# PReLU halves of the background rows merged by VectorE before the transposes, in a graph kernel on one core

## The reference

```
h = prelu(gcn_conv(x, W1, b1), a); h = prelu(gcn_conv(h, W2, b2), a)
x = layernorm(x + h)          # prelu(z) = z where z > 0, else a * z, with an own a for each feature
```

## The kernel before

| offset | engine | step |
|---|---|---|
| 0 | SyncE | `load` of the rows into X (L203) |
| 1 | TensorE | `transpose`, 4 transposes into bank 5 (L229) |
| 2 | ScalarE | `lift` to xt (L238) |
| 3 | TensorE | `mult_first`, 1 matmul (L243) |
| 4 | ScalarE | `rectify_first`: up = relu(z + b), down = relu(-z - b) (L252, L253) |
| 5 | TensorE | `mult_second`: 2 matmuls that add up, up by V2 and down by V2n = -a V2 (L261, L262); in slots jobs also h1 = up + (-a) down by 8 matmuls into bank 7 (L269, L270) |
| 6 | ScalarE | `rectify_second` (in slots jobs first H from bank 7), up and down again (L283, L284) |
| 7 | TensorE | `join`: xt + up + (-a) down by 12 matmuls into bank 7 (L295 to L297) |
| 8 | VectorE, ScalarE | `spread`: statistics (L309, L314, L316); `root` (L324) |
| 9 | VectorE, ScalarE | `invert` (L334, L335); `normal` (L344) |
| 10 | SyncE | `store` (L213); `store_h1` stands at offset 7 |

## Time and profile before

### The profile page before, as it was taken

The page is one execution under the profiler, slowest core; times in us unless marked ns, Lnnn a source line. Parts: engine busy times, 40 slices in busy tenths (PEclk is TensorE's granted clock), DMA queues, the critical chain, the costliest instruction groups (busy, mean ns, idle before and its releaser), DMA issues. The chain is left out here.

```text
span 12483.0 us, 94733 instructions
## 1 busy us (share of the span) xinstructions
PE 5282.3 (42%) x22640; PEld 4046.0 (32%) x22640; DVE 4400.5 (35%) x11160; ACT 3794.3 (30%) x11417; POOL 7315.7 (59%) x7464
## 2 busy tenths in 40 slices
PE   4510572444444444442044444455555553211533
PEld 3300351333323333331033333344444442111532
DVE  7900231232322223345033333334333333233433
ACT  3400461333222222226342222223222222124422
POOL 6777105326666666665655656666666666654556
PEclk7655555555665556655555555555555555555655
DMA  3211221133333333333133333333333333322211
GB/s 51 56 26 23 67 83 40 43 68 81 88 87 83 87 89 88 89 87 105 33 77 80 87 84 87 86 93 95 93 93 94 92 91 88 82 57 55 77 33 32
DMA packets 791340, 920.27 MB, mean 74 GB/s; under 512 B 258978, under 2 KB 676540, under 8 KB 790748
## 3 DMA queue, kind: packets, MB, share of 16 engines
q1 hardware_dynamic: 558638, 591.29, 16.0%
q0 software_dynamic: 232064, 323.36, 13.8%
q10 hardware_dynamic: 144, 0.10, 0.0%
HBM read 533.07 MB, written 388.06 MB: 74 GB/s over the span
## 5 line engine op out<-in xcount | busy, mean ns | idle before, releaser
L1589 POOL DMA_INDIRECT l_g<-tab,l x4704 | 4577.9, 973 | 2674.7 <-issue 1343.1
L1794 DVE TENSOR_TENSOR_SCAN l_w<-l_m,l_w,bank 96x512 f32<-96x512 bf16 x1248 | 1590.6, 1275 | 4299.7 <-remote 2331.8
L1626 PE MATMUL bank<-ident,l_w 96*128 96x96 f32 x5096 | 1085.3, 362 | 2341.3 <-DVE l_w L1794 1747.7
L1615 PE MATMUL bank<-ident,l_g 128*96 128x128 f32 x5096 | 1290.1, 401 | 1565.7 <-DMA l_g<-tab,l 665.5
L1689 ACT ACTIVATE l_o<-l_o,coef_d 128x96 f32<-128x96 f32 x2940 | 859.1, 363 | 3335.8 <-DVE l_o L1820 2135.7
L1626 PEld LDWEIGHTS bank<-ident,l_w 96*128 96x128 f32 x5096 | 850.8, 222 | 2611.7 <-DVE l_w L1794 1937.7
L1615 PEld LDWEIGHTS bank<-ident,l_g 128*96 128x96 f32 x5096 | 919.1, 191 | 1919.1 <-DMA l_g<-tab,l 710.4
L1685 ACT ACTIVATE l_o<-bank,coef_s 128x96 f32<-128x96 f32 x1764 | 454.5, 342 | 1998.7 <-remote 1453.1
L975 POOL DMA_INDIRECT XS<-in_x_dram,dst_i x196 | 198.3, 1012 | 709.8 <-DVEq L1319 647.1
L1820 DVE TENSOR_TENSOR l_o<-bank,T 128x384 f32<-128x384 f32 x735 | 392.6, 534 | 434.0 <-remote 389.1
L295 PE MATMUL bank<-ident,tail_xt 96*125 96x96 f32 (+1 forms) x1192 | 363.5, 405 | 295.8 <-ACT tail_down L284 219.4
(11 more groups left out here) (297 smaller groups left out, 11615.2 us busy)
## 6 DMA issues: line engine op xcount, KB each, us to landing
tab<-l_o SPq DMA_DIRECT2D x1176, 192.0 KB
l_g<-tab,l POOLq DMA_INDIRECT x4704
l_m<-mask_d SPq DMA_DIRECT2D x784, 96.0 KB
l_m<-mask_s SPq DMA_DIRECT2D x490, 96.0 KB
x3t<-XS SPq DMA_DIRECT2D x98, 192.0 KB
prep_x<-in_x_dram SPq DMA_DIRECT2D x100, 187.5 KB
x1t<-prep_a SPq DMA_DIRECT2D x100, 187.5 KB
x3d<-prep_b SPq DMA_DIRECT2D x100, 187.5 KB
```

The costliest lines, as they stand in the source:

```text
L1589: nc.gpsimd.indirect_dma_start(out=tile(G[q % RG], t), out_offset=None, in_=tables[0:table_at + (2 - p % 2) * TR, :] if p else first, in_o ...
L1615: last = nc.tensor.transpose(a_bank(q)[0:D, u:GE:U], G[q % RG][:, u * D:(u + 1) * D], self.ident[:, :])
L1626: last = nc.tensor.transpose(b_bank(q)[:, u * D:(u + 1) * D], W[q % RW][:, u:GE:U], self.ident[0:D, 0:D])
L1794: v.tensor_tensor_scan(out=W[q % RW][:, :], data0=masks[q % RM][:, :], data1=a_bank(q)[0:D, :], initial=W[(q - 1) % RW][:, GE - 1:GE] if q ...
```

## The change

VectorE merges the two halves of each PReLU while they are still transposed. After `rectify_first` it computes up = down * (-a) + up (`merge_first`). After `rectify_second` it does the same and then adds xt (`merge_second`, two instructions with a semaphore between them). `mult_second` is then one matmul in place of two, h1 is 4 transposes of up in place of 8 matmuls, and `join` is 4 transposes of up in place of 12 matmuls. The offsets become: merge_first 5, mult_second 6, rectify_second 7, merge_second 8, join 9, spread and root 10, invert and normal 11, store 12. The foreground is as it was.

```diff
-        n = due(7)
+        n = due(8)
         if kind == "sp" and n is not None and self.slots(n):
             self.store_h1(eng, n)
-        n = due(10)
+        n = due(12)
         if kind == "sp" and n is not None:
             self.store(eng, n)
-        n = due(7)
+        n = due(9)
         if kind == "pe" and n is not None:
             self.join(eng, n)
-        n = due(5)
+        n = due(6)
         if kind == "pe" and n is not None:
             self.mult_second(eng, n)
...
+        n = due(10)
+        if kind == "dve" and n is not None:
+            self.spread(eng, n)
         n = due(8)
         if kind == "dve" and n is not None:
-            self.spread(eng, n)
+            self.merge_second(eng, n)
+        n = due(5)
+        if kind == "dve" and n is not None:
+            self.merge_first(eng, n)
...
 def lift(self, act, n):
         if n >= 2:
-            act.wait_ge(self.joined, n - 1)
+            act.wait_ge(self.merged2, n - 1)
...
+    def merge_first(self, dve, n):
+        w = U * self.parts(n)
+        dve.wait_ge(self.rect1, n + 1)
+        self.nc.vector.scalar_tensor_tensor(out=self.up[:, 0:w], in0=self.down[:, 0:w], scalar=self.p.neg[:, 0:1],
+                                            in1=self.up[:, 0:w], op0=ALU.mult, op1=ALU.add).then_inc(self.merged1, 1)
...
 def mult_second(self, pe, n):
-        pe.wait_ge(self.rect1, n + 1)
+        pe.wait_ge(self.merged1, n + 1)
...
-        self.nc.tensor.matmul(z, self.p.v2[0:D, :], self.up[:, 0:w], start=True, stop=False)
-        self.nc.tensor.matmul(z, self.p.v2n[:, :], self.down[:, 0:w], start=False, stop=True).then_inc(self.second, 1)
+        self.nc.tensor.matmul(z, self.p.v2[0:D, :], self.up[:, 0:w], start=True, stop=True).then_inc(self.second, 1)
...
         for u in range(U):
-            o, c = self.p.bank[7][0:R, u * D:(u + 1) * D], slice(u * R, (u + 1) * R)
-            self.nc.tensor.matmul(o, self.up[:, c], self.p.ident[0:D, 0:D], start=True, stop=False)
-            last = self.nc.tensor.matmul(o, self.down[:, c], self.p.nd[:, :], start=False, stop=True)
+            last = self.nc.tensor.transpose(self.p.bank[7][0:R, u * D:(u + 1) * D], self.up[:, u * R:(u + 1) * R],
+                                            self.p.ident[0:D, 0:D])
...
+    def merge_second(self, dve, n):
+        w = U * self.parts(n)
+        dve.wait_ge(self.rect2, n + 1)
+        up, v = self.up[:, 0:w], self.nc.vector
+        self.link(dve, v.scalar_tensor_tensor(out=up, in0=self.down[:, 0:w], scalar=self.p.neg[:, 0:1], in1=up,
+                                              op0=ALU.mult, op1=ALU.add))
+        v.tensor_tensor(out=up, in0=up, in1=self.xt[n % 2][:, 0:w], op=ALU.add).then_inc(self.merged2, 1)
...
 def join(self, pe, n):
-        pe.wait_ge(self.rect2, n + 1)
+        pe.wait_ge(self.merged2, n + 1)
...
         for u in range(U):
-            o, c = self.p.bank[7][0:R, u * D:(u + 1) * D], slice(u * R, (u + 1) * R)
-            self.nc.tensor.matmul(o, self.xt[n % 2][:, c], self.p.ident[0:D, 0:D], start=True, stop=False)
-            self.nc.tensor.matmul(o, self.up[:, c], self.p.ident[0:D, 0:D], start=False, stop=False)
-            last = self.nc.tensor.matmul(o, self.down[:, c], self.p.nd[:, :], start=False, stop=True)
+            last = self.nc.tensor.transpose(self.p.bank[7][0:R, u * D:(u + 1) * D], self.up[:, u * R:(u + 1) * R],
+                                            self.p.ident[0:D, 0:D])
         last.then_inc(self.joined, 1)
```

More of the change, by code:

```diff
@@ L127, in __init__ @@
         self.mean = tmp("mean", [P, U])
-        names = ("landed", "turned", "lifted", "first", "rect1", "second", "rect2", "h1", "h1_kept", "h1_stored", "joined",
+        names = ("landed", "turned", "lifted", "first", "rect1", "second", "rect2", "merged1", "merged2", "h1", "h1_kept", "h1_stored", "joined",
                  "inner", "stats", "rooted", "inverted", "normed")
-        (self.landed, self.turned, self.lifted, self.first, self.rect1, self.second, self.rect2, self.h1, self.h1_kept,
+        (self.landed, self.turned, self.lifted, self.first, self.rect1, self.second, self.rect2, self.merged1, self.merged2, self.h1, self.h1_kept,
          self.h1_stored, self.joined, self.inner, self.stats, self.rooted, self.inverted, self.normed) = (
@@ L161, in turn @@
             self.transpose(eng, n)
-        n = due(9)
+        n = due(11)
         if kind == "act" and n is not None:
             self.normal(eng, n)
-        n = due(8)
+        n = due(10)
         if kind == "act" and n is not None:
             self.root(eng, n)
-        n = due(9)
+        n = due(11)
         if kind == "dve" and n is not None:
             self.invert(eng, n)
-        n = due(6)
+        n = due(7)
         if kind == "act" and n is not None:
```

## The result

The changed kernel took 12,648.13 us (median of four runs, 12,621.28 to 12,648.47) against 12,501.34 for the kernel before (four runs, 12,490.85 to 12,514.31): ratio 1.0119, interval 1.0103 to 1.0135. I had forecast 12,400 in a range of 12,200 to 12,640; the changed kernel is 147 us slower than the kernel before, and lies 8 us outside the range. The profiled execution took 12,648.11 us, 163.3 more than that of before.

The account below looks back on a forecast made before the run. GpSimd's gathers were taken as the floor, 1.24 us each, 30 us per six groups; only its waits beyond that could change. Terms -92 - 31 - 16 + 28 = -111 us gave 12,400 us, range 12,200 to 12,640.

Parts of the forecast that it names:

- (A): Smooth passes with nodes jobs: removing L262's two matmul pairs ahead of the turn that frees a tile, -92 us.
- (B): Smooth passes with slots jobs, and power passes: GpSimd's waits fall to 0.63 us per group, -31 and -16 us.
- (C): Merge instructions added to VectorE lengthen GpSimd's gathers, +28 us, with bounds +14 and +105.
- The rival built on that price: Gathers on GpSimd wait out VectorE's merges in full, 325 us instead of 28: +186, 12,697 us; chance 0.06.
- The rival of VectorE's queue: Merges queued ahead of VectorE's scans delay scans, TensorE and the next turn: +104, 12,615 us; chance 0.22.
- All waits go: Fewer TensorE pairs end all GpSimd's waits inside the passes with jobs: -757 us, 11,754 us; chance 0.12.
- Between the passes: GpSimd's wait for the last store before the next pass: -66 to +121 us in eight power passes, taken as 0.

Follow-up runs that it names:

- e9: Kernel before, with its old arithmetic and no merges, but its steps moved to the changed kernel's offsets: 12,660.92 us, ratio 1.0134.
- e8: Changed kernel with every step of a job but the load one slot later, on the slower chips: 12,310.65 us, ratio 0.9842.
- e11: Kernel before with every step of a job but the load one slot later, on the slower chips: 12,388.48 us, ratio 0.9910.
- e10: Kernel of e8 with the three merge instructions cut to one column, on the slower chips: 12,336.42 us, ratio 0.9871.
- e1: Same kernel as e8, on the faster chips: 10,208.02 us, ratio 1.0034 against the kernel before.
- e4: Kernel of e1 with the three merge instructions cut to one column, on the faster chips: 10,188.74 us, ratio 1.0011.
- e7: Kernel before, unaltered, run again for a second profile, on the slower chips: 12,469.43 us, one run.
- e2: Same kernel as e11, on the faster chips: 10,173.74 us, ratio 0.9999 against the kernel before.

## Why the prediction was wrong

**The step that failed** stands in two sentences of it. Of the join: "in the same cycle beside the load of tail_x, which decides its end; I cost their loss at nothing". And of the moved steps: "In each slot the semaphore waited for should be old [...] I cost all this at zero". I had the fact in hand, but read it only as a limit to the gain of a shorter join. The join was moved as well, out of the slot of the transposes, and `mult_second` into the slot just ahead of them. I asked of each moved step how old its own semaphore is, and not what stands behind the place that it leaves or takes. There stand the transposes, and the source of their wait had to be followed: SyncE's slot 0 lies behind a store that needs the turn back which TensorE issues just ahead of slot 1, so their semaphore is always new, and their wait is in the path of the turn behind them. e9, with the moves alone, costs +1.34% where I had 0; e8, with one slot more ahead of the transposes, turns the loss into -1.58%. None of my rivals had this path. No run tells which of the two moved steps costs how much.

**(A) and (B)** were of the right size for a kernel in which the load does not stand in the way. In e8 the waits fall from 263.7 to 237.7, from 245.9 to 147.6 and from 247.1 to 198.5 us: -173, where my terms had -16 - 92 - 31 = -139. But the cause that I gave to (A), L262's two pairs, does not hold up: e11 keeps these pairs and gains 85 of the 98 us with nodes jobs. That wait was the load's already, so the agreement of the -92 is luck. The sum was wrong besides: only 40 of a pass's 49 groups have a slot, so the five passes hold 33 jobs and not 40, and 2.3 us each give -77. Nor is TensorE always slow beside gathers, as I read it: the join's 24 pairs take 5.4 us from 9506.51 to 9511.94 in the trace of the kernel before, 0.23 us each, while GpSimd issues gather after gather, and the scan behind them starts 0.04 us after its turn's recorded end. The busy time that a slots job loses is 8.9 us (1213.0 to 796.5 over 47 jobs) and not 17: I had multiplied the mean length of records that overlap. With the load out of the way, the rest of the change (fewer matmuls, merges, other places) is worth the difference between e8 and e11, 12,310.65 to 12,388.48: 78 us.

**(C)** has the right size by luck. In e8 the gathers take 1.0 + 9.3 + 18.9 = 29 us more in the three stretches than before, against 28, and in the changed kernel 5; but much else differs between these. With the merges alone cut it is 52 us on kind A (e8 against e10) and 16 on kind B (e1 against e4). And only on kind B is it time: on kind A the run without merges is not faster, so +28 had no place in the sum. The merges take 739, 732 and 679 ns where I had 740 and 700. The Trainium skill ("SBUF — State Buffer", SBUF: two separate sides) has the loser of the shared port pair wait for the whole of the other's instruction, where a VectorE instruction with two SBUF inputs meets a GpSimd one that reads SBUF. With 149 x 2.15 = 320 us of merges, 52 and 16 us of longer gathers do not agree with a wait for all of it; whether the issue of a gather is such a reading instruction no run here shows. The rival built on that price did not come.

**The rivals.** The rival of VectorE's queue gave 12,615, near the measured 12,648, but its mechanism is not what happened: e9 is slower without any merge, e10 no faster with the merges cut. That 12,615 came within 33 us is luck. "All waits go" did not come in any run on kind A.

**Between the passes** the eight power passes wait 36.1 us more for stores, inside the -66 to +121 that I gave for phase; e8 has 15.6 less. I took zero, and it is a fifth of the loss. The kernel before itself has 9.6 us more there in its second profile (e7).

**Left open**: why e9 waits less than the kernel before with nodes jobs, and how the loss of the changed kernel divides between the lost cover of the join and the new place of mult_second. Either moved alone, the load's distance kept, would tell.

## What to carry to other kernels

Work that is removed or moved may have been the cover of something behind it: before an edit, ask of each instruction that stands behind the removed one what it waits for, and how late that is. In a schedule by slots, the age of a semaphore is not the difference of offsets: a DMA issued behind a store inherits the whole path of that store. When the arithmetic of a change is sound and the time is worse, try the distances first; on kind A one slot made 2.7%. And take a price from a run in which only the priced part is cut: the comparison with the kernel before agreed with my 28 us where the control gave 52 and 16. What shortens the instructions of an engine that waits anyway can come back as waiting.

## What the runs showed of the hardware that I had not expected

The same kernel takes 12,459 to 12,501 us on some chips and 10,154 to 10,176 on others, with the same gathers (973 ns mean in the first profile, 982 in e2) and a granted clock that does not differ (0.555 in e7, 0.551 in e2). What differs is how long a turn takes to reach its reader. On kind B the scan starts 0.04 us behind the recorded end of the turn (7406.56 + 1.09 to 7407.69); in e2 it is within 0.1 us for 82 to 90% of the scans of the three stretches, and never over 3.6. On kind A it is 4.7 us in the earlier trace rows and 0.04 us at 9609.16: in the profile of the kernel before some 30% of the scans are within 0.1 us, the medians are 0.8, 1.8 and 1.9 us, and the longest over 30. And GpSimd runs out of its seven tiles 73, 74 and 96 times in the 53, 33 and 47 jobs of the stretches. The Trainium skill ("Perfetto Trace Analysis", Tensor Engine Instruction) calls the recorded end of a matmul an estimate: on kind B the scans agree with it, on kind A some two thirds of them start later, so a wait recorded on TensorE may there be in part work still under way. Why the kinds differ was not found. It decides what a change is worth: the change is +1.2% on one and +0.5% on the other, the earlier load -1.6% and +0.3 to +0.4%.
